# Two groups of row loads at the end of a state-space projection stage, in another place of the sync engine's queue

## What is computed

```python
zxBCdt = x @ W_in.T                                 # x: 16 sequences, 64 tokens, layer-normed
z, xin, Bm, Cm, dt = jnp.split(zxBCdt, ...)         # 512, 512, 64, 64 and 8 columns
xin = silu(causal_conv4(xin))                       # per channel, 4 taps
xh = xin.reshape(Bsz, L, 8, 64)                     # 8 heads of 64 channels
dt = softplus(dt + dt_bias)
def step(h, ins):                                   # 64 steps, one after the other
    x_t, dt_t, B_t, C_t = ins
    h = exp(dt_t * A) * h + B_t * x_t               # the state h: heads x channels x 64
    return h, einsum('bhdn,bn->bhd', h, C_t)
y = (ys + xh * D) * silu(z)
return (y / rms(y) * norm_w) @ W_out.T
```

## Time and profile before

| What | Value |
|---|---|
| runs of the kernel before | 1522.17, 1523.06, 1528.12 us; median 1523.06 |
| span of the profiled execution, first to last instruction | 1519.6 us |
| the execution's own time outside the span | not told by the page; the median is 3.5 us above the span |
| PE / DVE / ACT / POOL busy, share of the span | 88% / 85% / 77% / 73% |
| stage `ssm_projections` | about 702 to 749.5 us |
| the scan's first matmul on PE | 753.20 us |

### The profile page before, as it was taken

One profiled execution on the slowest core, in us unless ns is written; L12 is line 12 of the kernel. 1 busy time (PEld: TensorE's weight loads), 2 busy tenths in 40 slices (PEclk: granted clock), 3 DMA queues, 4 the chain that ended last, 5 costly groups with the idle time before them and its releaser, 6 DMA issues. The chain is left out here.

```text
span 1519.6 us, 34485 instructions
## 1 busy us (share of the span) xinstructions
PE 1339.1 (88%) x12560; PEld 1001.5 (66%) x12560; DVE 1291.7 (85%) x1894; ACT 1163.9 (77%) x2975; POOL 1107.2 (73%) x1092
## 2 busy tenths in 40 slices
PE   5999999999999999978777777777777899999995
PEld 5888888888888888755333333333333678888884
DVE  4899999999999999987699999999999645666664
ACT  5888888888888888754699999999999235555552
POOL 2988888888888888754299999999999351443431
PEclk9999999999999999999899999999999999999998
DMA  4223131111111111005654110200000026888994
GB/s 135 59 74 103 45 85 49 39 46 38 46 44 38 48 42 31 2 2 132 163 89 80 17 32 1 35 14 1 2 1 1 1 68 261 311 303 308 307 310 139
DMA packets 106866, 132.99 MB, mean 88 GB/s; under 512 B 43274, under 2 KB 97617, under 8 KB 103256
## 3 DMA queue, kind: packets, MB, share of 16 engines
q1 hardware_dynamic: 96872, 61.61, 16.7%
q0 software_dynamic: 9840, 69.36, 12.8%
HBM read 110.47 MB, written 14.49 MB: 82 GB/s over the span
## 5 line engine op out<-in xcount | busy, mean ns | idle before, releaser
L565 POOL TENSOR_TENSOR half<-prob 128x512 f32<-128x512 f32 (+1 forms) x208 | 266.9, 1283 | 91.8 <-ACT prob L602 89.4
L597 ACT ACTIVATE prob<-ps_s,mx 128x64 f32<-128x64 f32 (+1 forms) x1040 | 239.1, 339 | 98.5 <-DVE prob L708 98.5
L1372 DVE TENSOR_TENSOR state<-ps_u,state 128x1024 f32<-128x1024 f32 x252 | 297.3, 1219 | 7.1 <-POOL state L1235 3.1
L701 DVE TENSOR_REDUCE mx<-ps_s 128x16 f32<-128x1024 f32 (+1 forms) x208 | 253.0, 1216 | 13.8 <-PE ps_s L648 12.3
L1330 PE MATMUL ps_y<-state,cz 128*32 128x256 f32 x2048 | 247.8, 384 | 1.8 <-DVE zs L1352 1.0
L648 PE MATMUL ps_s<-qbd,kT 64*128 64x256 f32 (+1 forms) x1664 | 221.1, 395 | 14.7 <-ACT prob L597 12.7
L708 DVE TENSOR_TENSOR prob<-ps_s,mx 128x192 f32<-128x192 f32 (+3 forms) x416 | 198.4, 518 | 7.2
L648 PEld LDWEIGHTS ps_s<-qbd,kT 64*128 64x128 f32 (+1 forms) x1664 | 147.8, 182 | 67.1 <-issue 38.5
L1330 PEld LDWEIGHTS ps_y<-state,cz 128*32 128x32 f32 x2048 | 109.1, 110 | 106.3 <-issue 30.0
L1312 PE MATMUL ps_u<-x_rows,b_diag 48*128 48x256 bf16 x1024 | 79.4, 275 | 112.0 <-DVE state L1372 105.0
L602 ACT ACTIVATE prob<-prob 128x704 f32<-128x704 f32 (+1 forms) x208 | 173.8, 836 | 0.0
(11 more groups left out here) (263 smaller groups left out, 3413.2 us busy)
## 6 DMA issues: line engine op xcount, KB each, us to landing
raw<-in_ctxT_dram SPq DMA_DIRECT2D x80, 268.0 KB, 2.8
x_rows<-ssm_x SPq DMA_DIRECT2D x96, 64.0 KB
raw<-in_ctxT_dram SPq DMA_DIRECT2D x16, 261.0 KB, 2.8
b_diag<-blank SPq DMA_DIRECT2D x2, 2048.0 KB, 8.9
slot_rows<-blank SPq DMA_DIRECT2D x1, 3483.0 KB, 15.4
xg<-slot_rows SPq DMA_DIRECT2D x27, 128.0 KB, 4.9
ssm_x<-xp SPq DMA_DIRECT2D x6, 384.0 KB, 3.9
back<-y_slots SPq DMA_DIRECT2D x8, 256.0 KB, 4.5
```

The source lines that it names most:

```text
L565: pool.tensor_tensor(half[0:rows, :, :], prob[0:rows, g % SLOTS, :, 0:L // 2], prob[0:rows, g % SLOTS, :, L // 2:L], ALU.add).then_inc(hal ...
L597: ins = nc.scalar.activation(prob[0:rows, g % SLOTS, h, :], part[:, h, :], ACT.Exp, bias=mx[0:rows, g % 2, h:h + 1])
L701: nc.vector.tensor_reduce(mx[0:rows, g % 2, :], part, AX_X, ALU.max, negate=True)\
L1372: nc.vector.tensor_tensor(h, flat(ps_u[k % 2][:, :, :]), h, ALU.add).then_inc(state_ready, 1)
```

## The change

In SP's part of `ssm_projections`, the row loads with i = 0 of both groups, each with its wait for a store, are written directly behind `store(HP)`. The copies of C, with their wait, and the stores of tiles 5, 6 and 7 come behind them. The waits at the end stay, and no other engine's code is touched.

```diff
             store(HP)
+            sp.wait_ge(x_stored[0], 16)
+            load_rows(sp, m, s, 0, x_loaded, groups=(0,))
+            sp.wait_ge(x_stored[1], 16)
+            load_rows(sp, m, s, 0, x_loaded, groups=(1,))
             sp.wait_ge(c_stored, 16 * NHI)
             for g in range(2):
                 sp.dma_start(m["CT"][:, g, :], ...).then_inc(copied_out, 16)
-            sp.wait_ge(x_stored[0], 16)
-            load_rows(sp, m, s, 0, x_loaded, groups=(0,))
-            for r in range(HP + 1, BP - 1):
+            for r in range(HP + 1, BP):
                 store(r)
-            sp.wait_ge(x_stored[1], 16)
-            load_rows(sp, m, s, 0, x_loaded, groups=(1,))
-            store(BP - 1)
             sp.wait_ge(copied_out, 16 * 5)
             sp.wait_ge(x_stored[2], 16 * (BP - 4))
```

## The result

The changed kernel takes 1525.67 us (median of 20 runs, 1523.91 to 1529.17), the kernel before 1522.35 (20 runs, 1518.71 to 1528.12). The ratio is 1.0022, with a 95% interval of 1.0014 to 1.0030: slower by 3.3 us (2.1 to 4.6). That lies inside the half per cent that was called no change and inside the range, but the forecast was 1.0 us faster, and the sign is clear.

What follows compares the result with a forecast made beforehand. No engine bounds the whole span; here group 1's late row loads delay PE's scan start. Opening estimates of -2.5, -1.2, -0.5 and +0.2 us gave -1.0, so 1523.06 - 1.0 = 1522.1 us, range 1519.4 to 1526.0.

Steps and rivals of the forecast that it cites:

- The place and the slack: End of ssm_projections: group 1's late row loads leave 3.63 us to win; SP was ready 0.4 us before ACT.
- The second wait at HP: SP's queue, between the groups' loads: SP stands 1.4 us for store HP; group 1's loads leave 1.8 us earlier.
- When the transfers land: After store HP's landing: twelve row loads take 6.0, 7.6 or 9.0 us at 131, 104 or 87 GB/s.
- the tail: After the last rows: half the copies and store 5 take 1.9 us, then 0.5 to 0.6 to the scan's opening.
- whole pieces: Landing summed from two trace stretches, 6.6 and 3.6 us: store 5 lands at 752.2, scan opens at 752.7, -0.5 us.
- The rival that came true: Block's end: SP's wait for store 5 behind twelve loads is the longer one; +0.2 to +1.3 us, chance 0.22.
- The third rival: Row loads' landing is set by the DMA engines alone; PE starts within 0.3 us of before, 1523.1 us, chance 0.12.
- the bounds of the landing: Scan's start: the early and late ends of the landing estimates give -2.5 to +0.6 us.
- The clock: Scan's start: full clock returning one pair sooner wins 1.7 us (1520.4), later loses as much; chance 0.08 together.

Runs made afterwards that it cites:

- act_queue: Changed kernel with the copies of C and store 5 issued from ACT's queue, behind its third and fourth gates; ratio to the kernel before 0.9997.
- needed_first: Changed kernel with both groups' row loads still in one piece, but behind the copies of C and store 5; ratio to the kernel before 0.9995.
- four_more: Changed kernel with four more 64 KB row loads, which nothing reads, ahead of the copies of C; ratio to the kernel before 1.0039.
- padded_after: Changed kernel with rows in DRAM 576 numbers apart instead of 512; one run, 21.50 us from first store's issue to PE's first scan matmul.
- wait_both: Changed kernel with the wait for store HP's landing moved ahead of group 0's loads, so all twelve enter an empty queue; ratio to the kernel before 1.0022.
- first_steps_end: Changed kernel's order with row loads halved to steps 0 to 3, the rest loaded at scan start, both store waits first; 1519.22 us, ratio to before 0.9975.
- first_steps: As first_steps_end, but with the copies of C and store 5 ahead of the half loads, as in needed_first; 1520.79 us, ratio to before 0.9986.

## Why the prediction was wrong

*What held.* The place and the slack: the late things are the rows and, once that is spent, SP's wait for store 5. The second wait at HP was met as worked out: group 1's loads left 7.9 us after the first store, forecast 7.6. After the landing of rows the copies and half of store 5 took 1.4 us (758.46 to 759.83), forecast 1.9; from there to the opening 0.5 us, forecast 0.5 to 0.6. The scan and what follows did not change: from PE's first matmul to the last output matmul 435.3 us after and 435.4 before, and from there to the end 330.8 and 331.0. In these two profiles a shift of the scan's start reaches the end whole.

*The step that failed* is "When the transfers land", the pace of the twelve loads. It was put at 104 GB/s, 7.6 us, with 87 as the worst, 9.0. From the landing of HP (742.23 + 5.0 = 747.2) to that of the last load it took 11.2 us (758.46), which is 70 GB/s. That is 3.6 us over the term, and 2.2 over its upper bound; with the tail half a microsecond shorter it moves the opening from the forecast 17.8 us after the first store to 20.97. The reason for the miss lies in how the bound was drawn: three windows of before, 87, 104 and 131 GB/s, were taken as the ends of the range, with the fastest of them from the same transfers, and none of them from twelve loads in one piece directly behind the stores. The "whole pieces" had the same fault, since they kept group 1's pace of before, six loads in 3.6 us. One reading of the kernel before would have warned: from HP's landing (742.0) to that of its last rows (753.16) it also took 11.2 us, although two stores and the end of the copies moved in that stretch as well. Taking these out of the way of the loads won nothing.

*The rival that came true* is the slower one, with the right mechanism (the block opens when store 5, behind twelve loads, has landed) at a chance of 0.22 and a price of +0.2 to +1.3. The traces of the changed kernel show +1.6 to +2.2 in S, the runs +3.3 (2.1 to 4.6). So 1.1 to 1.7 us of the medians' difference are not in S, nor, by the figures above, in the scan or behind it; where they lie stays open. Single profiles are too rough for it: up to the first store the changed kernel's two differ by 5.0 us, and behind the scan all kernels' profiles lie between 330.4 and 333.6. The third rival had half of the truth: the earlier issue did not move the rows' landing. That the measured median lies inside the stated range is owed to the room left there for noise; the bounds of the landing alone end at +0.6, 1523.7 us.

*Two waits in one.* In the changed kernel rows landed 0.3 us later than, or 0.3 us before, those of the kernel before, so the earlier issue won nothing, and the opening lost 1.9. act_queue and needed_first each take away only the second and are back at before; four_more lengthens only the second and loses 3.55 us of S; the half loads take both away and win. So the loss is the wait at the block's end, and the missing gain is the pace.

*What stays open* is why the loads run at 0.91 us in one place and at 0.55 to 0.69 in another. The one other row distance did not change it (padded_after), it is not what computes beside them (72 GB/s with every engine idle), the repeats don't show it as chance, an empty queue at the issue changed it little (wait_both), and the place behind the stores is not enough either, since half loads there ran at 0.70 for 64 KB (first_steps_end). In every kernel with whole loads issued from SP alone, though, the last rows landed 18.8 to 19.8 us after the first store, in whichever order. No run here settles it.

*The clock* changed nothing in the changed kernel: it stood at 1.2 GHz from 758.4 to 768.6, 10.2 us, as in the kernel before (752.5 to 762.8). In one variant it did. In first_steps_end PE begins 0.31 us behind the last gate, and the granted clock falls and returns earlier:

```profile
749.00:755.00 6.00, 2.63 (x22) 1.08 (x22) 2.36 (x2) 4.60 (x10) 1.30 (x2) 1.00 0.64 213
755.00:758.00 3.00, 3.00 (x16) 1.19 (x16) 2.36 (x2) 2.87 (x8) 1.16 (x1) 0.52 0.19 50
759.00:761.00 2.00, 1.85 (x17) 0.78 (x16) 1.97 (x3) 1.50 (x4) 2.00 (x3) 1.00 0.22 14
```

It is at 1.2 GHz for about 3 us here; in the kernel before for 753 to 762 whole:

```profile
753.00:762.00 9.00, 6.35 (x40) 2.59 (x40) 5.32 (x5) 3.16 (x8) 1.83 (x2) 0.50 0.23 17
```

From the first matmul to the last output matmul the scan takes 434.3 us there, before 435.4: 1.1 us that S does not tell. The other kernels fit: 434.4 in first_steps, whose low stretch is as short, 434.8 in needed_first and act_queue, where it lasts about 7 us. No run changes the clock alone.

## What to carry to other kernels

A transfer moved ahead in an in-order queue pushes back everything behind it, so look first for what a barrier needs from the part that is pushed back, and cost that wait at the slowest pace the moved transfers have shown, with a margin, not at a mean. A DMA that uses half of the engines holds back transfers that use all of them, on its own queue and, as the 9.6 us from ACT's queue show, on another one. Where the first steps of a loop need only a part of a load, cutting the load was worth more than any order of whole ones: S 16.24 against 18.90 us for the best order, and a ratio of 0.9975 against 0.9995, with intervals that just overlap.

## What the runs showed of the hardware

The same 64 KB row load took from 0.55 to 0.95 us in the runs here, at 68 to 131 GB/s where it ran alone, in different places of the queue. Issuing is not fixed either: the two copies of C took 2.16 us to issue before and 0.82 after, six row loads 2.0 to 3.6. A second issuing engine's queue did not shorten the landing of a store whose engines were taken (9.6 us from ACT's, 9.7 from SP's). And POOL, which issued six row loads in 3.68 us, ended the stage with a drain of 8.0 us, which was over 0.3 us after the last of its loads had landed.
